# Moving two whole-value products on TensorE and reading the experts' numbers 24 at a time in a two-layer kernel

## What is computed

```python
# layer 0
xn = layernorm(x)
q, k, v = split(xn @ W)              # each 256 wide
q, k = elu(q) + 1, elu(k) + 1
KV = k^T v  per batch row            # 8 rows of 1024 tokens, each KV 256 x 256
s = q @ KV / (q . sum(k) + 1e-6)     # the "values"
e = argmax(xn @ gate_w^T)            # one of 8 experts for a token
f = (relu(xn @ wg[e])**2 * (xn @ wu[e])) @ wd[e]
x = x + s * silu(f)
# layer 1
xn = layernorm(x)
... causal attention within blocks of 128 tokens, times W_out, plus b_out
... times silu of a layernorm with ln_g, ln_b
x = x + that
```

## Time and profile before

| | us |
|---|---|
| median of 3 runs | 509.84 |
| lowest and highest run | 509.61, 510.40 |
| the profiled execution, own time | 508.11 |
| its span, first to last instruction | 506.2 |

### The profile page before, as it was taken

How to read it: one execution, slowest core, us unless ns; L and a number is a source line. 1 busy time by engine, 2 the same in 40 slices (tenths; PEclk the granted TensorE clock), 3 DMA queues, 4 the chain that set the end, 5 groups by cost and what they waited for, 6 DMA issues and landing times.

```text
span 506.2 us, 11940 instructions
## 1 busy us (share of the span) xinstructions
PE 494.1 (98%) x3599; PEld 462.9 (91%) x3599; DVE 452.2 (89%) x1428; ACT 396.5 (78%) x910; POOL 320.4 (63%) x377
## 2 busy tenths in 40 slices
PE   6999999999999999999999999999999999999996
PEld 5999999999999999899999998888888898888885
DVE  6999999999999988969889949999999999999975
ACT  4878878787878784378888866788888888888885
POOL 5568876767676877454553028777877777877300
PEclk9999999999999999999999999999999999999999
DMA  7942322222222114558878563265665555655511
GB/s 221 258 126 86 124 84 84 85 84 84 85 85 84 43 53 167 160 170 246 249 231 260 180 206 119 69 145 128 139 147 126 141 131 132 142 139 126 105 42 64
DMA packets 59303, 67.70 MB, mean 134 GB/s; under 512 B 11880, under 2 KB 53616, under 8 KB 59248
## 3 DMA queue, kind: packets, MB, share of 16 engines
q1 hardware_dynamic: 44304, 38.69, 25.5%
q0 software_dynamic: 14944, 28.32, 22.4%
HBM read 39.85 MB, written 27.13 MB: 132 GB/s over the span
## 4 chain that ended last, share of the span: by engine, by line
PE 89%; POOL 3%; DVE 3%; DMA 2%; issue 2%; ACT 1%; SPq 0%; DVEq 0%; POOLq 0%
PE v_ps L1548 10%; PE q_ps L1526 10%; PE gu_ps L1183 6%; PE s_ps L1568 5%; PE y_ps L1202 3%; PE k_ps L171 3%; PE m_ps L171 3%; PE tq_ps L171 3%; PE m_ps L173 3%; PE m_ps L172 3%; PE k_ps L172 3%; PE t_ps L1159 3%; PE k_ps L173 3%; PE tq_ps L172 3%; PE tq_ps L173 3%; PE tq_ps L418 3%
## 5 line engine op out<-in xcount | busy, mean ns | idle before, releaser
L1972 POOL DMA_INDIRECT four<-expert_rows,gather_u x64 | 69.1, 1079 | 37.3 <-DMA expert_rows<-y 18.6
L978 POOL DMA_INDIRECT sorted_rows<-xn,row_u x64 | 67.6, 1057 | 17.2 <-issue 14.1
L967 POOL TENSOR_TENSOR xn<-xn 128x512 fp32r<-128x512 f32 x32 | 43.2, 1350 | 29.6 <-ACT xn L581 29.3
L1526 PE MATMUL q_ps<-xt,wqk 128*128 128x256 f32 x256 | 60.6, 379 | 0.0
L1548 PE MATMUL v_ps<-wvo,xt 128*128 128x256 f32 x248 | 58.7, 379 | 0.0
L1526 PEld LDWEIGHTS q_ps<-xt,wqk 128*128 128x128 f32 x256 | 48.5, 190 | 6.9 <-issue 0.4
L1548 PEld LDWEIGHTS v_ps<-wvo,xt 128*128 128x128 f32 x248 | 44.8, 190 | 4.8
L1978 POOL DMA_DIRECT2D res<-in_L_attn_x x26 | 34.9, 1341 | 19.0 <-DVE res L1775 17.3
L227 POOL DMA_DIRECT2D four<-sorted_rows x36 | 20.0, 555 | 39.8 <-PE t_ps L1159 35.0
L1688 ACT ACTIVATE xn2nd<-res,shift,rstd 128x256 f32<-128x256 f32 (+1 forms) x64 | 34.7, 594 | 7.9 <-DVE shift L1819 7.8
L171 PE MATMUL tq_ps<-xt,wq 128*128 128x256 f32 x128 | 38.4, 300 | 1.9 <-DVE xt L717 1.9
(11 more groups left out here) (292 smaller groups left out, 1791.9 us busy)
## 6 DMA issues: line engine op xcount, KB each, us to landing
expert_rows<-y SPq DMA_DIRECT2D x35, 256.0 KB, 3.4
four<-in_L_attn_x SPq DMA_DIRECT2D x32, 256.0 KB, 3.0
out_rows<-att SPq DMA_DIRECT2D x31, 256.0 KB, 2.1
res<-in_L_attn_x POOLq DMA_DIRECT2D x26, 256.0 KB, 4.9
four<-sorted_rows SPq DMA_DIRECT2D x36, 128.0 KB, 3.6
four<-sorted_rows POOLq DMA_DIRECT2D x36, 128.0 KB, 3.3
wdn<-in_L_ffn_wd SPq DMA_DIRECT2D x2, 512.0 KB, 6.8
sorted_rows<-res SPq DMA_DIRECT2D x8, 128.0 KB, 5.7
```

The lines of the kernel that those rows point to most:

```text
L967: nc.gpsimd.tensor_tensor(xn2[:, s, 1], xn[:, i], xn2[:, s, 0].bitcast(F32), ALU.subtract).then_inc(g["xn_split"], 1)
L978: nc.gpsimd.indirect_dma_start(out=z.sorted_dram.ap(), out_offset=bass.IndirectOffsetOnAxis(ap=row_u[:, i // CU, k:k + 1], axis=0), in_=xn ...
L1526: m = nc.tensor.matmul(q_ps[:, j, :], wqk[:, k, j * P:(j + 1) * P], xt[:, i % 2, k, :], start=(j == 0 and k == 0), stop=(k == KD - 1), ski ...
L1972: nc.gpsimd.indirect_dma_start(out=moe[:, n % SLOTS, t, :], out_offset=None, in_=z.expert_dram.ap()[0:(z.SLOTS - 1) * P, :], in_offset=bas ...
```

## The change

Three things. On TensorE, TAIL[1] is issued ahead of the sums of the last unit instead of behind them, and VectorE's `table_offsets(first_tiles)` ahead of `split_sums` instead of behind it. START[3] is issued in two halves, tile 0 ahead of `turn(0)` and tile 1 between `turn(0)` and `turn(1)`. And `load_owners` reads 24 numbers (`GROUP`) at a time: two loads in START[1], one in step 14, none elsewhere.

```diff
--- before.py
+++ after.py
@@ -178,18 +178,19 @@
     return z.res[:, z.UT * v:z.UT * v + z.UT, :].rearrange("p t d -> p (t d)").rearrange("p (k t) -> p k t", k=z.KD)
 
 
-def whole_values(nc, pe, z, p, banks, free, between=None):
+def whole_values(nc, pe, z, p, banks, free, between=None, only=None):
 
     v = ORDER[p]
     slot = WHOLE_ROWS.index(v // ROW)
     pe.wait_ge(z.kv_split, WHOLE_ROWS[slot] + 1)
     pe.wait_ge(z.rows_ready, z.UT * free)
-    for t in range(z.UT):
+    for t in range(z.UT) if only is None else (only,):
         for j in range(z.KD):
             m = nc.tensor.matmul(banks[:, t, 0:z.NV], parked(z, v)[:, j, t * P:(t + 1) * P], z.kvf[:, slot, j, :], start=(j == 0), stop=(j == z.KD - 1))
             if between and j == 0:
                 between(t)
-    m.then_inc(z.v_ready, 1)
+    if only != 0:
+        m.then_inc(z.v_ready, 1)
 
 
 def split_values(nc, pe, z, p, banks, free):
@@ -551,10 +552,10 @@
             run(pe, -1, step, UNITS - 1)
             whole_values(nc, pe, z, TAIL[0], tail_banks(TAIL[0]), SPLIT)
             count(UNITS, 0, 0)
-            sums(UNITS - 1, SLOTS - 1, UNITS // SLOTS - 1)
             pe.wait_ge(z.q_full, UNITS)
             pe.wait_ge(g["t_split"], UNITS)
             whole_values(nc, pe, z, TAIL[1], tail_banks(TAIL[1]), SPLIT)
+            sums(UNITS - 1, SLOTS - 1, UNITS // SLOTS - 1)
             pe.wait_ge(g["k_read"], UNITS)
             pe.wait_ge(g["base_moved"], CHUNKS)
             whole_values(nc, pe, z, TAIL[2], tail_banks(TAIL[2]), SPLIT)
@@ -939,8 +940,8 @@
             table_experts()
             table_changes()
             table_owners(first_tiles)
+            table_offsets(first_tiles)
             split_sums(UNITS + 1, 1, UNITS // SLOTS)
-            table_offsets(first_tiles)
             table_rows(first_tiles)
             divisors(TAIL[1])
             table_owners(other_tiles)
@@ -1042,11 +1043,11 @@
     END_PAIRS = {13 + 2 * e: e for e in range(len(END))}
     PAIRS = SLOTS // 2
     ROUNDS = PAIRS // QUAD
-    OWNERS, OCTET = 48, 8
+    OWNERS, OCTET, GROUP = 48, 8, 24
     STORE_LAG = 2 * QUAD + 1
-    OWNER_LOADS = {14: 48, 17: 56, 20: 64}
+    OWNER_LOADS = {14: 48}
     WEIGHT_TURNS = {PAIRS - 3 + f: (f,) for f in range(4)}
-    assert PAIRS == ROUNDS * QUAD and OWNERS + OCTET * len(OWNER_LOADS) == SLOTS
+    assert PAIRS == ROUNDS * QUAD and OWNERS + GROUP * len(OWNER_LOADS) == SLOTS
     assert z.B * z.L % P == 0
 
     def width(n):
@@ -1208,7 +1209,7 @@
             owners = [pe.alloc_register(f"owner{j}") for j in range(OWNERS)]
 
             def load_owners(first):
-                pe.load(owners[first % OWNERS:first % OWNERS + OCTET], z.owners_i[0:1, first:first + OCTET])
+                pe.load(owners[first % OWNERS:first % OWNERS + GROUP], z.owners_i[0:1, first:first + GROUP])
 
             def experts_of(n):
                 return [pe.snap(owners[(2 * n + u) % OWNERS], min_val=0, max_val=E - 1) for u in range(width(n))]
@@ -1241,17 +1242,17 @@
                 for f in WEIGHT_TURNS.get(m, ()):
                     turn_weight(f)
 
-            def values(p, before, owners_from=None):
-
-                load = owners_from is not None and (lambda t: load_owners(owners_from + t * OCTET))
-                whole_values(nc, pe, z, p, value_banks[p], before + 1, load)
+            def values(p, before, owners_from=None, only=None):
+
+                load = owners_from is not None and (lambda t: load_owners(owners_from + t * GROUP))
+                whole_values(nc, pe, z, p, value_banks[p], before + 1, load, only)
 
             values(START[0], TAIL[0])
             pe.wait_ge(z.first_sems["tables_made"], 2)
             values(START[1], TAIL[1], 0)
-            values(START[2], TAIL[2], 2 * OCTET)
-            values(START[3], START[0], 4 * OCTET)
+            values(START[2], TAIL[2])
             for i in range(2):
+                values(START[3], START[0], only=i)
                 turn(i, i, False)
             for m in range(PAIRS + 2):
                 step(m)
```

## The result

The changed kernel took 513.6 us (median of 12 runs, 511.21 to 514.56), the kernel before 509.8 us in the same session (12 runs, 508.99 to 511.84). The ratio is **1.0067, with a 95% interval of 1.0055 to 1.0079**: 2.8 to 4.0 us slower (the two medians lie 3.8 us apart). The forecast was 509.2 us, within 0.2% of before. The profiled execution took 512.97 us, its span is 511.1 us.

A forecast was written before the change was run, and what follows sets the result against it. TensorE, busy 98% of the span, was taken as the bound, so only filled holes or less work help. +0.04 us before the experts and -0.69 us in the loop gave -0.65 us, from 509.84 to 509.2 us; range 508.3 to 510.6 us.

The forecast's parts named there:

- I take 40 ns: Price per further number in TensorE's register loads, from singles and eights; sixteen more numbers cost 0.64 us per load.
- both ends, 29 and 125 ns: Lower and upper bound of the price per further number in a register load; forecasts 508.9 and 510.55 us.
- the other side: Rival that a register load's price is proportional to its numbers, deciding from 54 ns per number on; chance 0.13.
- the prediction's own sum: +0.04 us at the experts' first product and -0.69 us in the expert loop: -0.65 us.
- the moved product's 0.49 us: TAIL[1] ahead of the last sums fills their wait for VectorE, so TAIL[2] and START[1] begin 0.49 us earlier.
- the 2.3 us that three loads of eight were taken to cost: Expert loop: nine steps took 20.47 us against 18.18 us plain, so three loads cost 2.29 us.
- START[1], predicted 3.27 us: START[1] with two loads of 24: 1.75 + 0.41 + 0.64 + 0.47 us, from 208.19 to 211.46.
- The term was 0.41 + 0.64 = 1.05: First load in START[1]: the 0.41 us hole of before plus 0.64 us for sixteen more numbers.
- The term was 0.47: Second load in START[1]: 1.24 us behind 0.87 us of matmul work, plus 0.10 us to restart, leaves 0.47 us.
- Halves, predicted to fill the 0.49 us hole: START[3] in halves around the two turns takes 2.63 us and fills the 0.49 us hole before the first expert product.
- Loop, predicted -0.69 us: Expert loop: two of three loads go, saving 1.33 us; the one left grows by 0.64 us, saving 0.69 us.
- The rival "proportional": Loads cost 75 ns per number between products and 140 ns in the loop: +2.1 us together, 511.9 us; chance 0.13.

The follow-up runs named there:

- the kernel before profiled again: The kernel before with no edit, profiled and timed a second time: 510.2 us, ratio 0.9994 [0.9978, 1.0011].

## Why the prediction was wrong

**The step that failed** is "I take 40 ns, the nearest rows in size and place, so sixteen more numbers cost 0.64 us". Measured: 1.02 us in each of START[1]'s two loads. The slope came from 1 to 8 numbers and was used from 8 to 24, three times outside the rows. The text held both ends, 29 and 125 ns, and the point from which the other side decides, 54 ns. The likeliest value stood below that point, and 64 is above it. The forecast's range then used the 125 ns for the loop only, where one load of 24 in place of three of eight changed nothing that could be measured, and not in START[1], where two of them did.

This step turns the sign, but it isn't the whole miss. With 1.02 us in place of 0.64 in its three places, the prediction's own sum gives -0.65 + 1.14 = +0.5 us, an estimate, not the 3.4 us measured. Two more terms failed: the moved product's 0.49 us, which START[1] doesn't get, and the 2.3 us that three loads of eight were taken to cost. Both came from the one profile of before. What is left after them is told below.

Part by part, the change against the kernel before profiled again, which is the fairer partner:

- **START[1], predicted 3.27 us, took 4.24.** The structure was right. The first load has 1.58 us in the open (212.85 - 210.83, less 0.44 for the two records): 1.80 less only 0.22 of cover. The term was 0.41 + 0.64 = 1.05. The second has 0.84 us in the open (212.85 to 214.56, less 0.87): its 1.63, less 0.87 of cover, and 0.08 to restart. The term was 0.47, with the restart as 0.10. The size of the loads (0.38 and 0.39 us more than the 1.42 and 1.24 of the text) is 0.77 us of the miss of 0.97, lost cover and restarts the rest.
- **Moved product, predicted -0.49 us at START[1]: zero.** The gain is real up to START[0]. That begins 6.67 us after the last count (201.46 to 208.13), where it was 7.28 (201.38 to 208.66). But START[1] begins 9.37 and 9.40 us after it. It waits for ScalarE, whose rounding of the last keys and values stands ahead of the rows. ScalarE in the changed kernel, and in the kernel before again:

```profile
209.35 0.60 ACT L626 ACTIVATE kv_end<-m_ps 128x516 fp32r<-128x516 f32 x1 [3.67 <-PE m_ps L173]
209.85 0.83 ACT L219 ACTIVATE res<-tq_ps,zinv 128x256 f32<-128x256 f32 x2
```

```profile
209.31 0.60 ACT L625 ACTIVATE kv_end<-m_ps 128x516 fp32r<-128x516 f32 x1 [4.78 <-PE m_ps L173]
```

  The rounding starts 7.9 us after the last count in both, though the product it waits for ended 0.6 us earlier in the change. I had taken START[1] as free to start since the profile of before showed no wait there. Alone, the move was worth 0.9997.
- **Halves, predicted to fill the 0.49 us hole: they do in the change.** From START[3] to the first expert product are 2.62 us (216.82 to 219.44) against 2.63 predicted and 3.21 before. Alone they were worth 0.9993 [0.9982, 1.0004], which neither shows the half microsecond nor excludes it. The profile of that kernel shows nothing won: its second turn waits for its tile, where the prediction expected no such wait, and the first expert product comes 16.49 us after the last count, where the kernel before again has 16.50.

```profile
216.48 0.66 PE L1160 MATMUL t_ps<-ident,four 128*128 128x128 f32 x4 [0.31 <-DMA four<-sorted_rows]
```

- **Loop, predicted -0.69 us: nothing.** The load took 1.93 us and cost 1.69, close to the 1.76 of the text. What was wrong is the price of the three it replaced. The profile of before had caught them at 2.3 us; others have 1.8 and 0.5. From the first expert product to the last are 74.6 to 74.9 us in the four profiles with one load of 24 in the loop, and 73.4 to 75.4 us in the nine with three of eight.
- **The rival "proportional"** was the nearest, with its sign, its decision point and its 2.1 us. It was given 0.13. Its two prices, 75 and 140 ns, were too high and its place in part wrong: START[1] alone carries the loss.
- By the Trainium skill (Runtime: NRT & Kernel Launch, Instruction fetch mechanics: some 200 ns per register) a load of 24 would take 4.8 us, an estimate. The page gives the figure beside the register loads of a kernel's preamble. The loads here, from a table in SBUF, took 1.6 to 2.0 us, so it doesn't hold for them.

**What isn't accounted for.** By the profiles the change costs 17.98 - 16.50 = 1.5 us up to the first expert product and nothing in the loop. By the timed runs it is 3.4 us [2.8, 4.0], and 2.7 [1.6, 3.8] when repeated. That leaves about 1 to 2 us. The loads alone (4.0 us, 2.04 of it ahead of the first expert product by its profile, 18.54 us against 16.50) leave as much. They are also above START[1]'s loads alone (2.5) plus the loop's alone (-0.2), though the intervals of the first two touch.

Profiles show one place outside the edit that comes and goes by that much: a value product (`pa_ps`) at the second layer's start. In the kernel before again (waits view) and in the change (timeline) it waits for ScalarE's rows:

```profile
PE pa_ps L171 <- ACT res L218: 0.9, 1, 0.9
```

```profile
312.33 0.36 PE L171 MATMUL pa_ps<-kv_end,end_q 128*128 128x258 f32 x1 [0.93 <-ACT res L219]
```

In seven of the fourteen profiles it waits 0.9 to 1.6 us, in the other seven at most 0.3 us. From the last expert product to the end are 216.7 to 217.2 us in the former and 215.2 to 216.2 us in the latter. Of the four kernels with 24 in START[1] three have the wait (the one without it is START[1]'s loads alone), of the ten others four, the kernel before again among them. So it can hold the rest if the long loads make it more frequent; with one profile of each kernel that is a possibility and not shown. Up to the last count, ahead of the edit, the profiles spread by 2.3 us as well (199.70 to 202.02).

A lower clock is the other candidate. The changed kernel's runs have a mean granted TensorE clock of 0.991 or 0.992 of full speed (2.4 GHz) in six of the twelve (median 514.0 us), and 0.995 or more in the other six (512.6). When it was repeated one run of seven had 0.992, and none of the 26 of before beside it was under 0.994. But the clock isn't the bulk of it: the four runs with the loads alone had 0.995 to 0.998 and lost 4.0 us, and the changed kernel's own six without the lower clock are still 2.8 us above before. Whether the holes bring the lower clock about was not tried and stays open.

## What to carry to other kernels

Price a register load by a row of its own size: a slope from 1 to 8 numbers was a third too flat for 24. Then ask what has been issued ahead of it. Inside a product that has just waited on a semaphore, 1.58 us of a load of 1.80 were in the open; behind a product that had not begun to run, the same load left no hole. And profile the kernel before a second time before resting a sum on terms under a microsecond: of what this one rested on, a wait of 0.37 us was 0.61 us in the next profile of the same kernel, one of 0 was 0.21 us, and the three loads of the loop cost 2.3, 1.8 and 0.5 us in kernels alike in that stretch.

## What was unexpected of the hardware

A load of eight numbers on TensorE's queue takes 0.59 to 0.60 us between the products (minimum and median in each of six profiles; the longest, 0.78 us), but 0.59 to 1.2 us in the expert loop, and the same kernel shows both. ScalarE's rounding of the last keys and values waits only for TensorE's product by the program, yet began 1.07 and 1.09 us after the end of GpSimd's last scatter with the product early and with it late. The scatter in the changed kernel and in the kernel before again:

```profile
207.32 0.96 POOL L979 DMA_INDIRECT sorted_rows<-xn,row_u  x1 [0.30 <-issue]
```

```profile
207.26 0.96 POOL L978 DMA_INDIRECT sorted_rows<-xn,row_u  x1 [0.30 <-issue]
```

It ended at 208.28 and 208.22, and the rounding began at 209.35 and 209.31. In all the other profiles but one it was 1.04 to 1.12 us. The exception is the first profile of before: the rounding began at 207.13, only 0.64 us after the scatter's end (206.49) and 0.04 us after TensorE's product. So a fixed distance from the scatter isn't the rule. Whether the one holds the other was not tried.
